# Exponents of the state-space mixers bounded by a Relu pass of ScalarE instead of mask products on TensorE

## What is computed

```
A_d  = -exp(A_log) * softplus(dt + dt_bias)          # a step per token and head, never positive
L    = exp(segment_sum(A_d))                         # exp of the sum of steps between two tokens,
                                                     # 0 where the second token is the earlier one
M    = (C B^T) * L
Y    = M @ (dt * x)  +  what comes out of the carried state
```

## Time and profile before

| | |
|---|---|
| median of 3 runs | 2988.8 us (2985.39 to 2990.64) |
| the profiled execution | 2990.27 us, span 2988.6 us, mean granted TensorE clock 0.972 |
| TensorE | 2784.4 us busy, 93% |
| VectorE | 2020.4 us, 68% |
| ScalarE | 1249.0 us, 42% |
| GpSimd | 955.8 us, 32% |

### The profile page before, as it was taken

The page is one execution under the profiler, slowest core; times in us unless marked ns, Lnnn a source line. Parts: engine busy times, 40 slices in busy tenths (PEclk is TensorE's granted clock), DMA queues, the critical chain, the costliest instruction groups (busy, mean ns, idle before and its releaser), DMA issues. The chain is left out here.

```text
span 2988.6 us, 54351 instructions
## 1 busy us (share of the span) xinstructions
PE 2784.4 (93%) x19824; PEld 1846.6 (62%) x19824; DVE 2020.4 (68%) x3697; ACT 1249.0 (42%) x2098; POOL 955.8 (32%) x618
## 2 busy tenths in 40 slices
PE   6999999999999997995899999999999999997996
PEld 5677666666666764454666666666666666663443
DVE  4666666666566663377777777787777777775268
ACT  3344444334443431341454444544545444453242
POOL 2232223322233231242333333233333333323144
PEclk9999999999999997997999999999999999998898
DMA  4000000010000033144000000000000000013233
GB/s 127 15 29 21 21 21 21 21 34 22 21 21 24 19 113 141 43 155 181 11 23 22 21 21 14 21 21 21 14 14 21 21 21 21 11 62 133 93 108 132
DMA packets 80673, 140.16 MB, mean 47 GB/s; under 512 B 18120, under 2 KB 18632, under 8 KB 79568
## 3 DMA queue, kind: packets, MB, share of 16 engines
q1 hardware_dynamic: 70448, 126.44, 12.3%
q10 hardware_dynamic: 10144, 12.64, 1.4%
HBM read 104.98 MB, written 33.55 MB: 46 GB/s over the span
## 5 line engine op out<-in xcount | busy, mean ns | idle before, releaser
L613 PE MATMUL work<-b_xnT,shared_w 128*128 128x256 f32 x2304 | 548.6, 389 | 6.2 <-DVE b_parts L1125 6.1
L613 PE MATMUL work<-a_xnT,shared_w 128*128 128x256 f32 x2176 | 501.6, 386 | 6.1 <-DVE a_parts L1125 4.8
L613 PEld LDWEIGHTS work<-b_xnT,shared_w 128*128 128x128 f32 x2304 | 425.4, 191 | 89.4 <-issue 20.0
L613 PEld LDWEIGHTS work<-a_xnT,shared_w 128*128 128x128 f32 x2176 | 409.4, 192 | 78.2 <-issue 18.3
L1165 DVE TENSOR_TENSOR b_decay<-b_decay,b_gt 128x1024 f32<-128x1024 f32 x256 | 354.2, 1420 | 28.5 <-ACT b_decay L889 24.5
L889 ACT ACTIVATE b_decay<-seg 128x1024 f32<-128x1024 f32 x256 | 251.4, 1021 | 174.8 <-PE seg L739 174.0
L1375 POOL TENSOR_TENSOR a_y<-a_y,a_skip 128x1024 f32<-128x1024 f32 x32 | 103.4, 3231 | 513.8 <-DVE a_y L1154 513.8
L1340 POOL TENSOR_TENSOR b_rhs<-b_l_side,of_head 128x1024 fp32r<-128x1024 f32 x32 | 82.0, 2562 | 579.1 <-DVE b_l_side L1134 579.1
L841 ACT COPY shared_z<-work 128x256 f32<-128x256 f32 (+1 forms) x192 | 84.8, 442 | 414.3 <-PE work L613 414.3
L1044 DVE SCALAR_TENSOR_TENSOR shared_cv<-shared_pre,b_conv_w,shared_cv 128x256 f32<-128x256 f32 x480 | 222.4, 492 | 46.4 <-ACT shared_cv L835 38.6
L720 PE MATMUL work<-b_w_out,b_yz 128*128 128x512 f32 x512 | 226.8, 596 | 8.2 <-DVE b_y L1154 8.2
(11 more groups left out here) (314 smaller groups left out, 4523.6 us busy)
## 6 DMA issues: line engine op xcount, KB each, us to landing
shared_x<-in_L_attn_a_x SPq DMA_DIRECT2D x16, 512.0 KB, 3.7
a_x_res<-in_L_attn_a_x SPq DMA_DIRECT2D x32, 256.0 KB, 2.7
x_mid<-a_x_res SPq DMA_DIRECT2D x32, 256.0 KB, 2.0
shared_w<-in_L_ffn_d_w SPq DMA_DIRECT2D x2, 4096.0 KB, 12.9
f_d_w<-in_L_ffn_d_w SPq DMA_DIRECT2D x2, 4096.0 KB, 15.0
f_x_res<-x_mid SPq DMA_DIRECT2D x8, 1024.0 KB, 6.2
f_bc_w<-x_mid SPq DMA_DIRECT2D x8, 1024.0 KB, 5.6
shared_x<-x_mid SPq DMA_DIRECT2D x16, 512.0 KB, 3.6
```

Source lines behind the costliest of these rows:

```text
L613: mm = nc.tensor.matmul(dst, w_in[:, k, col:col + m], xnT[:, k, :], start=(k == 0), stop=(k == KD - 1))
```

## The change

The four products with the exponents stay, the sixteen mask products go. ScalarE takes two passes for each slot: `slot_bound` writes relu(-s) of the whole PSUM tensor into the slot's `decay` buffer and raises the new semaphore `seg_taken`, and `slot_exp` takes exp(-that) in place. The exponent is then at most 0, also above the diagonal, where the masked C B^T makes the product 0. TensorE's next unit waits for `seg_taken` in place of `exp_done`. On ScalarE both bounds of a unit stand ahead of its first exp, and so ahead of whatever stood between the two exps; in the first tile the first of the blocks behind a unit is copied between its exps. In mixer B the projection z2 is issued after the third unit of the second tile, ahead of `sums`, in place of after it. The mask constants, their DMAs and TensorE's wait for them go. The masks' SBUF is not used for anything else.

```diff
@@ seg_unit
-                    pe.wait_ge(exp_done, FREE + tile * NS + 2 * p)
+                    pe.wait_ge(seg_taken, FREE + tile * NS + 2 * p)
                     for k in range(4):
                         slot, half, r = unit_bank(p, k)
-                        nc.tensor.matmul(seg[k // 2][:, (k % 2) * 512:(k % 2 + 1) * 512], lhs[r:r + 32, p // 2, :],
...
-                    for b in range(3, -1, -1):
-                        for k in range(4):
-                            r, n = unit_bank(p, k)[2], 32 * (b + 1)
-                            out = seg[k // 2][32 * b:32 * b + 32, (k % 2) * 512:(k % 2 + 1) * 512]
-                            mm = nc.tensor.matmul(out.rearrange("p (h l) -> p h l", h=4)[:, :, 0:n],
-                                                  c["ident_bf"][r:r + 32, r:r + 32], c["masks"][r:r + 32, b, :, 0:n],
-                                                  start=False, stop=True, skip_group_check=True)
-                            if b == 0 and k % 2 == 1:
-                                mm.then_inc(seg_full, 1)
+                        mm = nc.tensor.matmul(seg[k // 2][:, (k % 2) * 512:(k % 2 + 1) * 512], lhs[r:r + 32, p // 2, :],
...
+                        if k % 2 == 1:
+                            mm.then_inc(seg_full, 1)
@@ the schedule of the gate inputs
         fill0, fill1 = spread(["dt"] + blocks, NS), spread(["z1", "z2"], NS)
+        if NP > 2:
+
+            fill1 = [[], [], [], ["z1"], [], ["z2"]] + [[]] * (NS - 6)
@@ ScalarE
-                def slot_exp(sec, j, s):
+                def slot_bound(sec, j, s):
+
+
                     tile = 2 * sec.i + j
                     act.wait_ge(seg_full, tile * NS + s + 1)
                     act.wait_ge(ydiag_done, FREE + 2 + tile * NS + s - 3)
                     nc.scalar.activation(decay[:, slot_buffer(j, s)].rearrange("p h l -> p (h l)"),
-                                         seg[s % 2][:, :], ACT.Exp).then_inc(exp_done, 1)
+                                         seg[s % 2][:, :], ACT.Relu, scale=-1.0).then_inc(seg_taken, 1)
+
+                def slot_exp(sec, j, s):
+                    tile = 2 * sec.i + j
+                    act.wait_ge(seg_taken, FREE + tile * NS + s + 1)
+                    d = decay[:, slot_buffer(j, s)].rearrange("p h l -> p (h l)")
+                    nc.scalar.activation(d, d, ACT.Exp, scale=-1.0).then_inc(exp_done, 1)
...
                     gate_silu(i)
+                    slot_bound(sec, 0, 0)
+                    slot_bound(sec, 0, 1)
                     slot_exp(sec, 0, 0)
...
                     for p in range(NP):
+                        behind = fill0[2 * p + 1] if nxt else []
                         if nxt:
                             fills(sec, fill0[2 * p])
                         if p + 1 < NP:
+                            slot_bound(sec, 0, 2 * p + 2)
+                            slot_bound(sec, 0, 2 * p + 3)
                             slot_exp(sec, 0, 2 * p + 2)
+                            fills(sec, behind[:1])
                             slot_exp(sec, 0, 2 * p + 3)
-                        if nxt:
-                            fills(sec, fill0[2 * p + 1])
+                            fills(sec, behind[1:])
+                        else:
+                            fills(sec, behind)
                     square(2 * i)
                     if nxt:
                         z_copy(sec, "z0a")
+                    slot_bound(sec, 1, 0)
+                    slot_bound(sec, 1, 1)
                     slot_exp(sec, 1, 0)
                     if nxt:
                         z_copy(sec, "z0b")
...
                         if p + 1 < NP:
+                            slot_bound(sec, 1, 2 * p + 2)
+                            slot_bound(sec, 1, 2 * p + 3)
                             slot_exp(sec, 1, 2 * p + 2)
                             slot_exp(sec, 1, 2 * p + 3)
```

More of the change, by code:

```diff
@@ L25 @@
 FLOOR = -104.0
-MASKED = -30000.0
 FREE = 2
@@ L159, in by_group, with build_constants @@
     return x.rearrange("(g t p) d -> g p t d", p=P, t=4)
-def build_constants(nc, ctx, ffn_w, mixers, weights, arena, mixer_signals, x_src, first_mixer_buffers):
+def build_constants(nc, ctx, ffn_w, mixers, weights, arena, mixer_signals, x_src):
     def sb(name, shape, dt=F32):
@@ L173, in build_constants @@
     c["root"] = sb("root", [P, 2])
-    c["ident_bf"] = sb("ident_bf", [P, P], BF16)
-    c["masks"] = sb("masks", [P, 4, 4, P], BF16)
-    c["masks_loaded"] = ctx.enter_context(nc.semaphore("masks_loaded"))
     c["of_head"] = sb("of_head", [P, 8])
@@ L222, in _ @@
             for t, v in (("ident", 0.0), ("tri_le", 1.0), ("tri_gt", 1.0), ("ones", 1.0), ("mean_w", 1.0 / DM),
-                         ("ident_bf", 0.0), ("masked_bf", 0.0), ("keep", 1.0)):
+                         ("keep", 1.0)):
                 step(nc.gpsimd.memset(c[t][:], v))
@@ L229, in _ @@
                                          base=0, pattern=[[-1, P]], channel_multiplier=1))
[L230 to L233, removed]
             step(nc.gpsimd.affine_select(out=c["tri_le"][:], in_=c["tri_le"][:], compare_op=ALU.is_ge, fill=0.0,
@@ L382, in mixer_phase @@
         seg_full = sig("seg_full")
+        seg_taken = sig("seg_taken")
         exp_done = sig("exp_done")
@@ L588, in _ @@
                 if later:
[L589 to L592, removed]
                     with nc.allow_non_contiguous_dma(reason="small vectors"):
@@ L728, in seg_unit @@
                     pe.wait_ge(rhs_ready[p // 2], tile + 1)
-                    pe.wait_ge(exp_done, FREE + tile * NS + 2 * p)
+                    pe.wait_ge(seg_taken, FREE + tile * NS + 2 * p)
                     for k in range(4):
                         slot, half, r = unit_bank(p, k)
-                        nc.tensor.matmul(seg[k // 2][:, (k % 2) * 512:(k % 2 + 1) * 512], lhs[r:r + 32, p // 2, :],
-                                         rhs[p // 2][r:r + 32, 4 * half:4 * half + 4, :].rearrange("p h l -> p (h l)"),
-                                         start=True, stop=True)
-                    for b in range(3, -1, -1):
-                        for k in range(4):
-                            r, n = unit_bank(p, k)[2], 32 * (b + 1)
-                            out = seg[k // 2][32 * b:32 * b + 32, (k % 2) * 512:(k % 2 + 1) * 512]
-                            mm = nc.tensor.matmul(out.rearrange("p (h l) -> p h l", h=4)[:, :, 0:n],
-                                                  c["ident_bf"][r:r + 32, r:r + 32], c["masks"][r:r + 32, b, :, 0:n],
-                                                  start=False, stop=True, skip_group_check=True)
-                            if b == 0 and k % 2 == 1:
-                                mm.then_inc(seg_full, 1)
+                        mm = nc.tensor.matmul(seg[k // 2][:, (k % 2) * 512:(k % 2 + 1) * 512], lhs[r:r + 32, p // 2, :],
+                                              rhs[p // 2][r:r + 32, 4 * half:4 * half + 4, :].rearrange("p h l -> p (h l)"),
+                                              start=True, stop=True)
+                        if k % 2 == 1:
+                            mm.then_inc(seg_full, 1)
                 def ydiag_slot(tile, j, s):
@@ L799, in _ @@
                 run(prologue(), pro_steps[-6:])
-                pe.wait_ge(c["masks_loaded"], 16 * 16)
                 run(first(), schedule(False, True))
@@ L961, in supertile @@
                         silus(sec)
-                for s in (xnT_ready, tap_ready, z_ready, silu_done, xt_ready, bt_ready, exp_done, sq_done, e3_ready):
+                for s in (xnT_ready, tap_ready, z_ready, silu_done, xt_ready, bt_ready, seg_taken, exp_done, sq_done,
+                          e3_ready):
                     act.sem_inc(s, FREE)
@@ L1996, in build @@
         weights = {"a": part("L0_attn_a_"), "b": part("L0_attn_b_")}
-        first = ExitStack()
         arena = arenas(nc, ctx)
[L2000 to L2004, removed]
+        c = build_constants(nc, ctx, part("L0_ffn_"), (mixer_a, mixer_b), weights, arena, mixer_signals, x0)
         for k, stage in enumerate(STAGES):
@@ L2007, in build @@
             if stage == "A":
-                with first:
-                    mixer_phase(nc, mixer_signals, ffn_signals, mixer_a, c, arena, mixer_b, psum, src, dst, weights["a"])
+                mixer_phase(nc, mixer_signals, ffn_signals, mixer_a, c, arena, mixer_b, psum, src, dst, weights["a"])
             elif stage == "B":
```

1 line of the change is left out of this document (removed).

## The result

The kernel before takes 2986.35 us here (median of 8 runs, 2983.41 to 2990.64), the changed kernel 2994.9 us (8 runs, 2994.48 to 3004.35). The ratio is 1.0032, 95% interval 1.0022 to 1.0041: slower by 0.3%. The forecast was 2993.8 us and +0.17%. Its number was good, but the sum behind it is not: a cost that it doesn't have and gains that it has too small or not at all nearly cancel. The way there is by the periods of the supertiles, a period being the time from the first exponents of one to those of the next.

The account below looks back on a forecast made before the run. TensorE's in-order queue was taken to bound both mixers. Up to 51 us of mask savings go into two waits per supertile: A +17, B -12, sum +5 on 2990.3, median 2993.8 us; range 2976 to 3008.

Parts of the forecast that it names:

- lower bound: TensorE's mask removal: 0.22 us saved a unit, if 0.1 us must still be paid when leaving the exponents.
- upper bound: TensorE's mask removal: 0.32 us saved a unit, if leaving the exponents costs what it does now, 0.44 us.
- bad end of +0.04: ScalarE's exp reading SBUF instead of PSUM: nothing much changes, at worst +0.04 us a pass.
- Passes don't overlap: Rival, ScalarE in both mixers: a pass costs 1.02 us instead of 0.92, +18 us, 3012 us; chance 0.14.
- A, the new wait: Mixer A, second tile: yoff1a waits for z0b's copy behind three ScalarE passes, +1.04 us a supertile, +14.6 for 14.
- 1.5 us for VectorE's later products: Mixer A's first supertile: exps 1.84 us later delay VectorE's products; 1.5 taken, plus 1.3 for z0b, +2.8.
- everything behind yoff1a moves along with it: Mixer A, TensorE's queue: yoff, rt0, out0 and the projections start later with yoff1a's +1.04 us.
- the 0.8 of the forecast: Mixer B, wait before yoff1a: idle time of TensorE's loads there about 0.8 us more.
- VectorE's late products at the tile's end: Mixer B, second tile: state1b still waits for parts; ydiag only 0.9 to 1.0 us earlier, masks alone over 1.6.
- B keeps more: Rival, mixer B: VectorE's sides and state1b aren't late, 0.8 us more kept a supertile, -12, 2982 us; chance 0.18.

Follow-up runs that it names:

- one_pass: Changed kernel without the exps, one Relu pass per slot in the old kernel's places (output not the reference's); 2938.51 us, ratio 0.9839 to the kernel before.
- longer_wait_B: Changed kernel with two unused ScalarE passes behind the bounds of mixer B's second tile, ahead of the copy of z0b; 3056.62 us, ratio 1.0216.
- short_filler_A: Changed kernel with one unread 512-column product on TensorE during the wait before yoff1a, mixer A only; 2979.55 us, ratio 0.998.
- z0b_early: Changed kernel with z0b copied between the two bounds of the second tile's first unit, in both mixers; 2948.28 us, ratio 0.9866.
- z2_back: Changed kernel with mixer B's projection z2 back at its old place behind sums; 3015.89 us, ratio 1.01.
- filler_A: Changed kernel with three unread 512-column products on TensorE during the wait before yoff1a, mixer A only; 3004.41 us, ratio 1.005.

## Why the prediction was right, and where it was not

**The saving.** Of the bounds 0.22 and 0.32 us a unit I took 0.27; it is 0.32: the next instruction stands 0.44 us behind the exponents, and one_pass gets 48 of the 51 us. The rule on the drain at a change of tiling mode, in the Trainium skill (TensorEngine Tiling, Key Properties), spoke for the lower bound. The rows don't bear that bound out: the next product stands 0.44 us behind the exponents with the masks and without them. Whether a drain is part of these 0.44 us no run here shows. A reading behind the upper bound was wrong: the output projection is eight products of 512 columns (`KE` = 8), each run as two instructions, and not sixteen. The 0.44 us are the length of one such instruction, 7.13 / 16, and the bound stands.

**ScalarE.** Pairs of bounds take 1.94 us, as forecast; a pass in place has a mean of 1074 ns against 1021, at the bad end of +0.04. The table loads stayed at 32 + 32. That agrees with the Trainium skill (ScalarE: Activation LUTs, "Table sets: the hidden batching unit"), by which relu is in every set. "Passes don't overlap" is out: from the first bound at 244.29 to the copy at 247.06 three passes take 2.77 us, 0.92 each.

**A, the new wait: right.** Forecast +1.04 us a supertile, measured +1.14 (68.26 to 69.40), with TensorE's idle time 1.54 and that of its loads 1.81. The first supertile cost +0.9, not +2.8: the projection behind `parts` starts 18.58 us after the first exponents (81.93 - 63.35), where before it was 18.68 (82.82 - 64.14), so the 1.5 us for VectorE's later products are not in this trace. But one trace doesn't settle this term: longer_wait_B, whose code in A is the same, has 74.77 us there, +2.5, and its first exponents take 0.80 us where they take 0.50 here, at a mean clock of 0.70 against 0.76 up to 80 us. In both TensorE waits 3.93 us for `parts`, where the earlier trace rows have 4.75:

```profile
81.93 17.63 PE L603 MATMUL work<-a_xnT,shared_w 128*128 128x256 f32 x72 [3.93 <-DVE a_parts L1127]
```

**A, the clock: missing.** The step that failed is the sentence that everything behind yoff1a moves along with it. It moves, and in 9 of 15 supertiles it also gets slower. A's supertiles 2 to 15 came out at +33.3 us, of which the wait explains 14 x 1.14 = 16; short_filler_A, which has the wait and not the fall, has 971.07 us for the same 14, +15.9. The other 17.4 are clock: the nine projections are 15.7 us over 9 x 7.13, and a first tile of the last of these supertiles took 1.7 longer than the others (38.70 against 37.02 to its second exponents). The granted clock of each window was there to be read, and the forecast takes it as a constant: it moves the projection along with its 7.13 us unchanged.

**B: right in sign, too small.** Forecast -1.25 us a supertile, measured -1.69: eight units give 2.5 (one_pass), and the wait at yoff1a takes 0.8 back (z0b_early against the changed kernel), which is the 0.8 of the forecast. The mis-sized terms are the saving (8 x 0.05 = 0.4). VectorE's late products at the tile's end cost next to nothing, because z2 covers them; z2_back shows 1.13 us a supertile without that cover. The first supertile gave -1.5 where +0.4 was forecast. The last is ScalarE's, as forecast: pairs follow each other at 3.83 us (2699.40 to 2703.23) where they followed at 3.05.

```profile
2697.32 1.94 ACT L873 ACTIVATE b_decay<-seg 128x1024 f32<-128x1024 f32 x2 [4.32 <-PE seg L722]
...
2699.14 2.00 ACT L880 ACTIVATE b_decay<-b_decay 128x1024 f32<-128x1024 f32 x2
2699.40 0.51 PE L722 MATMUL seg<-b_rhs,b_lhs 32*128 32x512 f32 x4 [1.11 <-ACT b_decay L873]
...
2703.23 0.51 PE L722 MATMUL seg<-b_rhs,b_lhs 32*128 32x512 f32 x4
```

Up to the end of its last output projection it takes 67.6 us instead of 64.0, +3.6 where +5 was forecast, at a mean clock of 0.90 instead of 0.97, so part of even this is clock. The feed-forward stage behind it, which has no edit, takes 1.1 us less, and the two together give +2.5.

**The sum.** Forecast +17 - 12 = +5. Measured in A +16.8 without the clock and +17.4 for it; -6.8 in the last supertile of A and the feed-forward stage, where -0.3 was forecast; -22.7 in B; -0.8 at the start: +3.9. The total was right since the clock's 17 us stood against 11 us more in B and the 6.8 us, most of which is a fall of the clock in the kernel before. That these nearly cancel is luck: the new wait and B's direction were forecast, the closeness of the number was not earned. Without the fall of the clock the kernel takes 2979.6 us (short_filler_A), close to the 2982 of the rival "B keeps more".

## What to carry to other kernels

When a pass is added to an in-order engine, look for the small copy behind it on which another engine waits, and move the copy ahead: that was worth 1.7% here, some five times the loss. When an edit puts a wait of one to three microseconds on TensorE in front of a dense group, as the waits of 1.19 to 2.62 us here, price the group at both clock levels, not only the wait. And read a saving by the instruction that follows the removed group, not by its durations: here 0.76 less 0.44 us, which came back whole.

## What the hardware showed that I had not expected

- An empty TensorE queue can slow the products that come after it. Slow projections of the 15 in A, by the wait before yoff1a: none with none (before, z0b_early), 1 at 0.59 us, 7 at 1.19 (masks kept), 9 at 1.54, 15 at 2.49, none when the queue was filled. Each costs 1.4 to 1.7 us, and some 3 us where it takes 10 us.
- The same wait gives 7.13 us in one supertile and 8.56 in the next. With 69.4 and 70.8 to 71.1 us in a sequence that nearly repeats after three supertiles, the place in time may decide. In longer_wait_B all of A from the second supertile on lies 2.5 us later and the same nine are slow; no run moved the supertiles alone, so it stays open. In A's last supertile TensorE waits 1.67 us before `rs0` in the kernel before and loses its clock, and waits 1.87 there in the changed kernel and keeps it (projections of 9.80 and 7.13 us).
- In B, 1.68 us of wait left the clock up in all 15 supertiles, and 2.62 brought it down in all. yoff1a has 1.98 us of products in B and 1.20 in A; whether that is the reason stays open.
- Useless products of 1.12 us in each of 15 waits made the kernel 15 us faster.
- A product of 512 columns from the fp32 `ident` and `w_in` is two instructions and 0.95 us. So is one of the output projection: eight products in sixteen instructions, 7.13 / 8 = 0.89 us each. The price of 0.43 in filler_A was that of one instruction.
- ScalarE's pass of 1024 elements takes 1029 ns out of PSUM and 1074 in place in SBUF.
